# Kept operands of the first layer on ScalarE's queue: a two-batch gated mixture of dense nets with a category layer on one NeuronCore

## The reference

```python
s0 = relu(x @ swi[0]) @ swo[0]                  # 512 -> 2048 -> 512
s1 = relu(x @ swi[1]) @ swo[1]
eo = relu(x @ wi[type_label]) @ wo[type_label]
gate_in = concatenate([eo[:, 0], s0[:, 0], s1[:, 0]], axis=-1)
w = softmax(relu(gate_in @ g1) @ g2)            # 3 weights for each batch
x = x + eo * w[0] + s0 * w[1] + s1 * w[2]
x = x + x @ W[category] + b[category]
```

## Time and profile before

| | us |
|---|---|
| median of 3 runs | 1934.02 (1933.66 to 1934.57) |
| the profiled execution | 1933.93 |
| its span | 1931.9 |
| TensorE busy in the span | 1927.0 |
| VectorE busy | 1356.0 |
| ScalarE busy | 980.0 |
| GpSimd busy | 344.8 |

### The profile page before, as it was taken

One profiled execution on the slowest core, in us unless ns is written; L12 is line 12 of the kernel. 1 busy time (PEld: TensorE's weight loads), 2 busy tenths in 40 slices (PEclk: granted clock), 3 DMA queues, 4 the chain that ended last, 5 costly groups with the idle time before them and its releaser, 6 DMA issues. The chain is left out here.

```text
span 1931.9 us, 25225 instructions
## 1 busy us (share of the span) xinstructions
PE 1927.0 (100%) x8494; PEld 1593.8 (82%) x8494; DVE 1356.0 (70%) x1523; ACT 980.0 (51%) x1441; POOL 344.8 (18%) x245
## 2 busy tenths in 40 slices
PE   9999999999999999999999999999999999999999
PEld 8888888888888888888888888888888888888887
DVE  8999999998666556665655545589976666555566
ACT  7666756766553334444554344456566434344342
POOL 0221132123111111331111111111321112111120
PEclk9999999999999999999999999999999999999999
DMA  6868777867877666886776676587788677656652
GB/s 234 326 251 325 288 293 269 310 242 306 295 250 232 205 217 186 279 290 228 243 253 212 202 225 197 194 287 290 268 304 282 221 234 226 213 183 213 223 158 99
DMA packets 193314, 470.91 MB, mean 244 GB/s; under 512 B 17060, under 2 KB 58020, under 8 KB 187044
## 3 DMA queue, kind: packets, MB, share of 16 engines
q1 hardware_dynamic: 192900, 468.52, 71.1%
q10 hardware_dynamic: 288, 0.79, 0.1%
HBM read 322.44 MB, written 146.80 MB: 243 GB/s over the span
## 5 line engine op out<-in xcount | busy, mean ns | idle before, releaser
L1765 PE MATMUL rps<-HH,WD 128*128 128x512 f32 x2672 | 876.8, 389 | 0.0
L1765 PE MATMUL ups<-XH,WU 128*128 128x512 f32 x2632 | 864.7, 389 | 0.3 <-DMA WU<-wu_kept 0.3
L1765 PEld LDWEIGHTS rps<-HH,WD 128*128 128x128 f32 x2672 | 501.6, 188 | 104.7 <-issue 0.5
L1765 PEld LDWEIGHTS ups<-XH,WU 128*128 128x128 f32 x2632 | 493.9, 188 | 104.5 <-issue 0.9
L1765 PE MATMUL rps<-HL,WD 128*128 128x512 f32 x1336 | 519.9, 389 | 0.0
L1765 PE MATMUL ups<-XL,WU 128*128 128x512 f32 x1316 | 512.2, 389 | 0.0
L802 POOL TENSOR_TENSOR HT<-hid 128x512 f32<-128x512 f32 x81 | 111.2, 1373 | 1349.2 <-PE rps L1765 1349.2
L1311 DVE TENSOR_TENSOR HL<-HT,HH 128x1024 fp32r<-128x1024 f32 x240 | 290.0, 1217 | 11.4 <-ACT HH L988 6.3
L1333 DVE SCALAR_TENSOR_TENSOR ACC<-rps,gw,ACC 128x1024 f32<-128x1024 f32 x126 | 161.5, 1282 | 192.7 <-PE rps L1765 192.5
L1765 PEld LDWEIGHTS rps<-HL,WD 128*128 128x128 f32 x1336 | 250.7, 188 | 52.1
L1765 PEld LDWEIGHTS ups<-XL,WU 128*128 128x128 f32 x1316 | 247.1, 188 | 51.2
(11 more groups left out here) (155 smaller groups left out, 1530.9 us busy)
## 6 DMA issues: line engine op xcount, KB each, us to landing
WU<-wu_kept SPq DMA_DIRECT2D x448, 256.0 KB, 3.6
WD<-wd_kept SPq DMA_DIRECT2D x224, 512.0 KB, 3.5
wd_kept<-WD SPq DMA_DIRECT2D x112, 512.0 KB, 4.0
wu_kept<-WU SPq DMA_DIRECT2D x30, 1024.0 KB, 4.9
wu_kept<-WU SPq DMA_DIRECT2D x30, 768.0 KB, 4.1
sums_kept<-ACC SPq DMA_DIRECT2D x28, 512.0 KB, 6.0
MB<-sums_kept SPq DMA_DIRECT2D x28, 512.0 KB, 5.6
XS<-in_x_dram SPq DMA_DIRECT2D x20, 512.0 KB, 6.2
```

What stands on the lines that cost most here:

```text
L1765: ins = pe.matmul(dst, stationary[a], moving[c], start=start and j == 0, stop=stop and j == 2, skip_group_check=True)
```

## The change

`load_up` moves from SyncE's list to ScalarE's. It now loads operand 0 alone and then the pairs 1 and 2, 3 and 4, 5 and 6, each with one DMA of 512 KB, requested when the later product of the pair is done. The number of its requests falls from 448 to 256, and the semaphores from seven to four. TensorE waits for the pair of the operand. In ScalarE's list the loads of the next half stand behind `first_product`, `chain`, `relu_22` and `relu_12` of a half.

```diff
+PAIRS = 4
...
-        s_wu = [sem(f"up_operand_loaded_{i}") for i in range(PRODUCTS)]
+
+        s_wu = [sem(f"up_operands_loaded_{i}") for i in range(PAIRS)]
...
-            def load_up(n, i):
-                late = int(i >= EARLY)
-                sp.wait_ge(s_up, PRODUCTS * (n - 1) + i + 1)
-                sp.wait_ge(s_wuk[late], 16 * PREP_HALF[n])
-                if weight_set(n // 2) == 0:
-                    sp.wait_ge(s_wsk, 64)
-                sp.dma_start(WU[:, i, :, :].bitcast(F32),
-                             wu_kept[2 * weight_set(n // 2) + n % 2, :, i, :, :]).then_inc(s_wu[i], 16)
...
-                        if n + 1 < HALVES and not prepared_half(n + 1):
-                            load_up(n + 1, j % PRODUCTS)
...
+            def load_up(n, i):
+
+                if n >= HALVES or prepared_half(n):
+                    return
+                late = int(i >= EARLY)
+                part = slice(max(i - 1, 0), i + 1)
+                act.wait_ge(s_up, PRODUCTS * (n - 1) + i + 1)
+                act.wait_ge(s_wuk[late], 16 * PREP_HALF[n])
+                if weight_set(n // 2) == 0:
+                    act.wait_ge(s_wsk, 64)
+                act.dma_start(WU[:, part, :, :].bitcast(F32),
+                             wu_kept[2 * weight_set(n // 2) + n % 2, :, part, :, :]).then_inc(s_wu[i // 2], 16)
...
                 if m < STEPS - 1:
                     first_product(a)
+                    load_up(a + 1, 0)
...
                     if more:
                         chain(a)
+                        load_up(a + 1, 2)
...
                     if more:
                         relu_22(a)
+                        load_up(a + 1, 4)
...
                     if more:
                         relu_21(a)
                         relu_12(a)
+                        load_up(a + 1, 6)
...
-                    pe.wait_ge(s_wu[i], 16 * (n - PREP_HALF[n] + 1))
+                    pe.wait_ge(s_wu[(i + 1) // 2], 16 * (n - PREP_HALF[n] + 1))
```

More of the change, by code:

```diff
@@ L1203, in _ @@
                     relu_12(a)
+                    load_up(a + 1, 6)
                     first_product(b)
+                    load_up(b + 1, 0)
                     hidden_high(d, 5)
@@ L1237, in _ @@
                     chain(b)
+                    load_up(b + 1, 2)
                 for ms, c, stage in mixing[1]:
@@ L1247, in _ @@
                     relu_22(b)
+                    load_up(b + 1, 4)
                 if m in (1, 2):
@@ L1258, in _ @@
                     relu_12(b)
+                    load_up(b + 1, 6)
                 if gating:
```

## The result

| | before | changed |
|---|---|---|
| median of 17 runs each, us | 1934.28 (1933.66 to 1936.41) | 1939.38 (1936.75 to 1941.73) |
| ratio | | 1.0023 (95%: 1.0016 to 1.0029) |
| profiled execution, us | 1933.93 | 1937.28 |
| its span, us | 1931.9 | 1935.4 |

The change made the kernel 0.23% slower, 5.1 us by the medians, and its runs scatter five microseconds. The forecast of 1933.6 us and its range up to 1935.4 us were wrong. The profiled execution is one of the quicker ones, so its trace shows only 3.5 of the 5.1 us.

What follows compares the result with a forecast made beforehand. The prediction took TensorE, busy in 1927.0 of 1931.9 us, to bound the kernel. It summed 1933.93 - 0.5 (boundary stalls gone) + 0.2 (new tokens' transfer) = 1933.6 us, with a range of 1932.9 to 1935.4 us.

Steps and rivals of the forecast that it cites:

- The stalls that go: TensorE's waits for late up operands at two boundaries, 0.43 and 0.1 us, would vanish: gain about 0.5 us.
- ScalarE's requests: ScalarE's 256 requests at 0.4 us, 102 us on top of 980 us busy, hide in its idle time: cost 0.
- The added waits and the pairs: ScalarE's added semaphore waits, and operands 1, 3 and 5 waiting for their neighbour, would each cost 0.
- my 15 us of room: From product 2's end to the next half's product 1: 15 us, against 12.1 us for late request plus longest landing.
- The new tokens' transfer: New tokens land 0.8 us late at two boundaries against 0.37 us of slack: 0 to 0.4 us lost, taken as 0.2.
- Cost in the plain steps: 0: In plain steps, 1.17 us of ScalarE idle time ahead of a copy hides a 0.4 us request, so nothing is lost.
- The sign of being wrong that I had named: TensorE waiting over a microsecond in all for a hidden block, `XL`, copies or `WU`, or plain-step busy share under 100%.
- TensorE's 100% in the windows: TensorE busy 797.00 of 797 us (483 to 1280) and 440.00 of 440 us (1450 to 1890), read as transfers not slowing matmuls.
- The rule: Skill's rule: requests from several engines share 16 DMA engines, saving only initiation time; alone it gives 0, the trace 0.5 us.
- The slower one that I wrote: ScalarE held at its requests ahead of the copy at three boundaries, 1.9 us lost at each: 1939 us; chance 0.03.
- New small stalls: At the boundaries, late tokens or slow ScalarE requests cost TensorE up to 1.1 us each: up to 1935.6 us; chance 0.15.
- The range: From 1932.9 us (stalls gone, runs 0.36 us below the median) to 1935.4 us (most of the small stalls).

Runs made afterwards that it cites:

- the boundary experiment: The kernel before, with only the up operands of halves 24 to 27 and 72 to 75 requested from ScalarE, one by one: 1935.00 us, ratio 1.0002.

## Why the prediction was wrong

*The stalls that go* (0.5 us): right. No wait for `WU`, and the growth at the boundaries is -0.1 and -0.5 us. The pair 1 and 2 of half 73 was requested at 1416.7 (forecast: 1415).

*ScalarE's requests* (0 on the path): right in the change, for a partly wrong reason. I added 102 us to ScalarE's 980 us busy, and named a busy time within 10 us of 980 as a sign. That sign was empty, since requests are not counted as busy. A request took 0.33 us at the median (all of line 975: issue in ns, at the least, the median, the most). 254 of the 256 ran while ScalarE was at an activation, as that of 1033.50 beside the copy of 1033.44, so they took little of its time.

```profile
L975 ACTq DMA_DIRECT2D WU<-wu_kept x256: 326/326/393, 430.9 to 1868.2; - x128
```

Where two stand together ahead of a tight chain they do cost, as the boundary experiment shows.

*The added waits and the pairs* (0): right on ScalarE's queue for TensorE's wait for `WU`, which was all that I costed of the pairs. The pairs on SyncE's list show what my 15 us of room rested on: the request coming soon after the product. Behind the store it comes late, and 2.0 us are lost at each boundary.

*The new tokens' transfer* (0 to 0.4 us, taken as 0.2 in all): the right mechanism, at the wrong place. I shared out the engines by bytes between the two queues for `XT` at the two boundaries, and for nothing else. The copy at the last boundary came with 0.2 us of waiting in the weight loads alone and no idle time of TensorE.

*The step that failed* is "Cost in the plain steps: 0", with the sentence it leaned on, that transfers beside the matmuls do not slow them. I looked at TensorE and ScalarE in a plain step and costed the change's effect on them. I never asked which transfers of SyncE's list somebody waits for. In the trace of before, VectorE's waits held 41 us for `MX` and 24 us for `MB`, all hidden, with TensorE's product 6 a microsecond behind:

```profile
DVE MX L1426 <- DMA MX<-in_x_dram: 22.8, 4, 5.9
DVE MX L1429 <- DMA MX<-in_x_dram: 18.0, 2, 12.0
...
DVE MX L1426 <- DMA MB<-sums_kept: 16.0, 4, 4.9
...
DVE MX L1429 <- DMA MB<-sums_kept: 7.8, 1, 7.8
```

The sum needed a term "mixing operands 1 to 2.6 us later at six or seven places, less 1.0 us of slack". It measured 3.6 us in one profile and 6.5 us in the other. The sign of being wrong that I had named came: TensorE waits for a hidden block (`block_22`) by 1.6 us in all. I read TensorE's 100% in the windows as slack; it only says that nothing had yet run out of slack.

*The rule.* I weighed that several queues interleave on the same engines as a rule that would take my gain away. It should have been put to the other transfers. The trace agrees with it in that sense: the two queues fill 51.9 + 18.8 = 70.7% of the engines' span where the one filled 71%, so no bandwidth was won: the same busy time is now split between the two queues. The Trainium skill, DMA: Bandwidth & Descriptors, section Queues, rings and completion order, says that each DMA engine takes turns between the queues with work, packet by packet. `MX` landing 2.6 us later beside a pair load requested at the same moment agrees with that. How the queues share out the engines in between, no run here shows.

*The rivals.* The slower one that I wrote had ScalarE held at its requests. It happened nowhere in the change. "New small stalls" had the right kind of loss, TensorE behind tokens that land late, but the wrong place (the boundaries) and too small a size: up to 1935.6 us, where 1939.4 was measured.

*The range.* By its own terms it would begin at 1933.0 (1933.4 less 0.36) and not at 1932.9. This changes nothing in the outcome.

## What to carry to other kernels

Moving a load to a second queue takes away its turn behind the others. Here the transfers on the first queue then landed later (`MB` 6.8 in place of 5.6 us, `MX` 5.8 in place of 4.8), `MX` the more so the larger the load beside it. Before such a move, list the transfers that an in-order engine waits for, even where the wait is hidden, and the slack of what stands behind them in its list. And put an operation that the bounding engine needs ahead of one that waits for a transfer; here that one reordering made the change harmless.

## What the runs showed of the hardware that I had not expected

- A DMA request on ScalarE, of 0.33 us, ran beside an activation in 254 of 256 cases in the changed kernel. Two together took 1.20 and 1.42 us ahead of the gate in the boundary experiment and held the next operation by 0.27 and 0.58 us.
- Of two stalls of 2.0 us in one execution, one was followed by some 3.3 us at the lower clock level (granted 0.78 and 0.80 over 8 us) and one was not.
- Beside a 512 KB load on the other queue, a 256 KB slice requested 0.5 us ahead of it landed in 5.6 us in place of 4.5, and one requested at the same moment in 7.4 in place of 4.8. Beside two loads of 256 KB the like slices took 5.0 and 5.4 us, and with the 512 KB load 4 us later 4.3 and 4.6.
